# Token-outermost block transposes, a strided stationary operand, and one scattered row set per slot, in a two-layer gated cross-attention kernel

## The reference, cut to what matters

```python
# second attention: 16 heads of width 128, 8 key/value heads, softmax over 128 context tokens
scores = jnp.einsum('bhtd,bhsd->bhts', q, k) / scale
attn   = jax.nn.softmax(jnp.where(mask, scores, -jnp.inf), axis=-1)
out    = jnp.einsum('bhts,bhsd->bhtd', attn, v).transpose(0, 2, 1, 3).reshape(B, T_text, N_HEADS * HEAD_DIM) @ Wo
x = x + jnp.tanh(g_xattn[1]) * out
# second feed-forward: one shared expert, and 8 routed experts of which each token takes the best two
rw, sel = jax.lax.top_k(probs, 2)
x = x + jnp.tanh(g_ffn[1]) * (shared_out + sparse_out)
```

## Time and profile before

| | value |
|---|---|
| median of 3 runs | 1303.56 us (1302.22 to 1304.45) |
| the profiled execution: its own time | 1302.48 us |
| its span in the trace | 1300.7 us |
| PE busy | 1240.1 us, 95% |
| PE weight loads busy | 1098.9 us, 84% |
| DVE busy | 894.9 us, 69% |
| ACT busy | 738.5 us, 57% |
| POOL busy | 549.1 us, 42% |
| mean granted clock of PE | 0.989 |

### The profile page before, as it was taken

How to read it: one execution, slowest core, us unless ns; L and a number is a source line. 1 busy time by engine, 2 the same in 40 slices (tenths; PEclk the granted TensorE clock), 3 DMA queues, 4 the chain that set the end, 5 groups by cost and what they waited for, 6 DMA issues and landing times. The chain is left out here.

```text
span 1300.7 us, 23370 instructions
## 1 busy us (share of the span) xinstructions
PE 1240.1 (95%) x7907; PEld 1098.9 (84%) x7907; DVE 894.9 (69%) x2453; ACT 738.5 (57%) x2053; POOL 549.1 (42%) x542
## 2 busy tenths in 40 slices
PE   6899999999999989999999989999999988999998
PEld 4788888888888878888888888899988977888987
DVE  6678788887988776743433346657687776788857
ACT  4777787777877743322222247666565653546542
POOL 3564456644565533200000001866668675223430
PEclk9999999999999989999999999999999998999999
DMA  7000000000000310398100011434343355413434
GB/s 266 10 1 1 9 1 1 1 9 0 0 0 1 74 31 2 113 326 245 64 0 1 1 18 49 142 112 136 100 138 130 115 179 166 118 45 99 129 100 174
DMA packets 85672, 101.09 MB, mean 78 GB/s; under 512 B 16985, under 2 KB 72802, under 8 KB 85186
## 3 DMA queue, kind: packets, MB, share of 16 engines
q1 hardware_dynamic: 82162, 90.45, 23.1%
q0 software_dynamic: 3408, 9.34, 2.0%
HBM read 53.60 MB, written 46.18 MB: 77 GB/s over the span
## 5 line engine op out<-in xcount | busy, mean ns | idle before, releaser
L98 PE MATMUL bank<-wvo_hi,pc_hi_a 128*128 128x256 f32 x512 | 149.7, 292 | 6.5 <-DVE pc_lo_a L1337 5.7
L1748 ACT ACTIVATE act_g_f<-bank 128x512 f32<-128x512 f32 x64 | 38.2, 598 | 190.9 <-PE bank L100 190.9
L100 PE MATMUL bank<-wvo_hi,pc_lo_a 128*128 128x256 f32 x512 | 144.8, 283 | 0.0
L99 PE MATMUL bank<-wvo_lo,pc_hi_a 128*128 128x256 f32 x512 | 144.6, 283 | 0.0
L1807 DVE TENSOR_TENSOR hid_f<-act_g_f,bank 128x512 f32<-128x512 f32 x64 | 44.0, 688 | 142.3 <-ACT act_g_f L1748 142.3
L877 ACT ACTIVATE probs_a<-bank,nbias_a,q_r_a 128x128 f32<-128x128 f32 x256 | 114.4, 472 | 23.7 <-DVE nbias_a L995 23.4
L140 POOL TENSOR_TENSOR rstd<-mv,half 128x4 f32<-128x4 f32 x12 | 12.2, 1020 | 260.7 <-DVE mv L135 260.7
L1055 POOL TENSOR_TENSOR probs_a<-probs_a,rden_a 128x512 f32<-128x512 f32 x64 | 66.6, 1041 | 103.8 <-DVE rden_a L1001 103.8
L98 PEld LDWEIGHTS bank<-wvo_hi,pc_hi_a 128*128 128x128 f32 x512 | 98.2, 192 | 12.5 <-DVE pc_lo_a L1337 8.3
L1277 ACT ACTIVATE probs_a<-probs_a,nmin_a 128x128 f32<-128x128 f32 x256 | 99.5, 392 | 7.7 <-DVE nmin_a L1321 7.4
L99 PEld LDWEIGHTS bank<-wvo_lo,pc_hi_a 128*128 128x128 f32 x512 | 98.5, 192 | 3.2
(11 more groups left out here) (314 smaller groups left out, 4139.9 us busy)
## 6 DMA issues: line engine op xcount, KB each, us to landing
rows_in<-blank_f SPq DMA_DIRECT2D x8, 2193.0 KB, 21.1
staged<-blocks_a SPq DMA_DIRECT2D x32, 512.0 KB, 2.9
turned_a<-staged SPq DMA_DIRECT2D x128, 128.0 KB, 2.9
xs_raw_f<-rows_in SPq DMA_DIRECT2D x39, 129.0 KB
y_tok_f<-rows_out SPq DMA_DIRECT2D x4, 1024.0 KB, 8.9
we_raw<-in_L_ffn_We_gate_up SPq DMA_DIRECT2D x2, 1408.0 KB, 9.9
ctx_raw_a<-in_ctx SPq DMA_DIRECT2D x8, 256.0 KB, 3.0
x_sb<-in_x SPq DMA_DIRECT2D x4, 512.0 KB, 10.1
```

Source lines behind the costliest of these rows:

```text
L98: nc.tensor.matmul(out, w[0], x[0], start=start, stop=False)
L99: nc.tensor.matmul(out, w[0], x[1], start=False, stop=False)
L100: return nc.tensor.matmul(out, w[1], x[0], start=False, stop=stop)
```

## The change

Four things are changed, all in the second attention and the routing.

1. `blocks` and `turned` hold a block's 128 columns as (token, head), head innermost. TV therefore writes each element four words (16 bytes) behind the one before. Th and Tl become plain copies of 128 x 512 without rearrangement. The columns of `pt`, of C's result and of `pc` are now (token, head), and W's stationary operand for head h is every fourth element of `pc`.
2. SC is one indirect DMA for a word, not two. Groups 0 and 1 have their eight words in slots 35 to 42 and in slots 51, 52, 53 and 58 to 62; before they had them in pairs in slots 35 to 38 and 51 to 54. Group 2's eight words stay in slot 0 of the feed-forward stage and group 3's in slot 7.
3. Group 2's routing (`hurried`) stands earlier from NA on: RT, RL and RS by one slot, all other words by two (the last, PL, at 29 instead of 31).
4. The last unit's TV stands at the end of slot 57, before SH; before it stood in slot 58, behind SH.

The diff, cut to its core:

```diff
@@ second_order
     routing = {15: "E0", 17: "E1", 20: "NA0", ...
-               30: "RQ0", 32: "RQ1", 33: "RK0", 34: "PL0 PL1", 35: "SC0", 36: "SC1", 37: "SC2", 38: "SC3"}
-    hurried = {15: "E0", 17: "E1", 20: "NA0 NA1", 21: "NA2 NA3 NM0", 22: "NB0 NB1", 23: "NB2 NB3", 24: "NX0 NX1", 25: "RT0 RL0", 26: "RS0",
-               28: "RQ0", 29: "RQ1", 30: "RK0", 31: "PL0 PL1"}
+               30: "RQ0", 32: "RQ1", 33: "RK0", 34: "PL0 PL1"}
+    scatter = [{35 + n: f"SC{n}" for n in range(8)}, {51: "SC0", 52: "SC1", 53: "SC2", 58: "SC3", 59: "SC4", 60: "SC5", 61: "SC6", 62: "SC7"}]
+    hurried = {15: "E0", 17: "E1", 18: "NA0 NA1", 19: "NA2 NA3 NM0", 20: "NB0 NB1", 21: "NB2 NB3", 22: "NX0 NX1", 24: "RT0 RL0", 25: "RS0",
+               26: "RQ0", 27: "RQ1", 28: "RK0", 29: "PL0 PL1"}
...
-        unit(v - 1, "TV")
+        if v < U:
+            unit(v - 1, "TV")
...
+        for r in range(2):
+            words(scatter[r].get(s, ""), r)
         unit(s, "Ch", "Cl")
...
+        if v == U - 1:
+            unit(v, "TV")
         words(following.get(s, ""))
@@ second_attention
-        pc = pair("pc", [P, 2, QH, P])
+        pc = pair("pc", [P, 2, P, QH])
...
-                        last = three_pass(nc, out_of(b), [v[:, n % 2, h, :] for v in pc], [v[:, j * QH + h, :] for v in w["vo"]],
+                        last = three_pass(nc, out_of(b), [v[:, n % 2, :, h] for v in pc], [v[:, j * QH + h, :] for v in w["vo"]],
...
-                    nc.vector.transpose(blocks[:, p % 2, :, n % 2, :].rearrange("p j (h t) -> p h j t", h=QH),
+                    nc.vector.transpose(blocks[:, p % 2, :, n % 2, :].rearrange("p j (t h) -> p h j t", h=QH),
...
-                    nc.gpsimd.tensor_copy(pt[0][:, n % 2, :].rearrange("p (h i t) -> p i h t", h=QH, i=4),
-                                          turned[:, n // 2 % 2, :, n % 2, :].rearrange("p i (h t) -> p i h t", h=QH)).then_inc(sem("pt_hi_ready"), 1)
+                    nc.gpsimd.tensor_copy(pt[0][:, n % 2, :].rearrange("p (i x) -> p i x", i=4), turned[:, n // 2 % 2, :, n % 2, :]).then_inc(sem("pt_hi_ready"), 1)
@@ Router.gpsimd_step
-            b = m * GB + i
+            b, r = m * GB + i // 2, i % 2
             pool.wait_ge(self.places_ready, m + 1)
-            for r in range(2):
-                self.scatter(self.pay[:, b, :], self.row_of[:, r, b:b + 1], self.rows_in[:, :], self.rows_sent)
+            self.scatter(self.pay[:, b, :], self.row_of[:, r, b:b + 1], self.rows_in[:, :], self.rows_sent)
```

More of the change, by code:

```diff
@@ L1367, in _ @@
                         pool.wait_ge(sem("c_filled"), n - 1)
-                    nc.gpsimd.tensor_copy(pt[0][:, n % 2, :].rearrange("p (h i t) -> p i h t", h=QH, i=4),
-                                          turned[:, n // 2 % 2, :, n % 2, :].rearrange("p i (h t) -> p i h t", h=QH)).then_inc(sem("pt_hi_ready"), 1)
+                    nc.gpsimd.tensor_copy(pt[0][:, n % 2, :].rearrange("p (i x) -> p i x", i=4), turned[:, n // 2 % 2, :, n % 2, :]).then_inc(sem("pt_hi_ready"), 1)
                 elif name == "Tl":
                     pool.wait_ge(sem("pt_hi_ready"), n + 1)
-                    hi, lo = (v[:, n % 2, :].rearrange("p (h i t) -> p i h t", h=QH, i=4) for v in pt)
-                    nc.gpsimd.tensor_tensor(lo, turned[:, n // 2 % 2, :, n % 2, :].rearrange("p i (h t) -> p i h t", h=QH), f32(hi),
-                                            ALU.subtract).then_inc(sem("pt_ready"), 1)
+                    hi, lo = (v[:, n % 2, :].rearrange("p (i x) -> p i x", i=4) for v in pt)
+                    nc.gpsimd.tensor_tensor(lo, turned[:, n // 2 % 2, :, n % 2, :], f32(hi), ALU.subtract).then_inc(sem("pt_ready"), 1)
         return {"weights_used": (sem("w_done"), U), "scores_read": (sem("min_ready"), U), "probs_read": (sem("pt_ready"), U),
@@ L2136, in routed_feed_forward @@
     extras = {
[1 row of a table removed]
+        0: ["NB 3 0", "NB 3 1", "NB 3 2", "NB 3 3", *(f"SC 2 {n}" for n in range(8))],
         1: ["X 1 0", "X 1 1", "SD 0", "SD 1", "SD 2"],
@@ L2143, in routed_feed_forward @@
         6: ["RK 3", "SE 2", "SE 3"],
[1 row of a table removed]
+        7: ["PL 3 0", "PL 3 1", *(f"SC 3 {n}" for n in range(8)), "SE 4"],
         8: ["TB 0"],
```

## The result

| | before | after |
|---|---|---|
| median | 1303.56 us (1302.22 to 1304.87, 5 runs) | **1371.3 us** (1369.46 to 1373.46, 5 runs) |
| span of the profiled execution | 1300.7 us | 1371.7 us |
| mean granted clock | 0.989 | 0.989 |

The ratio is 1.0522, 95% interval 1.0508 to 1.0537: the change costs 68 us. I had forecast 1293, range 1286 to 1310. The second attention carries 70.0 of the 71.0 us between the two spans. Its first C starts at 815.94 us before and 816.94 after, and the next stage's first matmul, which ends it, at 1108.56 and at 1179.52: 292.6 and 362.6 us. The feed-forward stage behind it lasts 192.1 and 192.2 us.

What follows compares the result with a forecast made beforehand. PE, busy 95% of the span, was taken as the bound. From 1302.48 us, -1.8 (group 0's scatters), -10 (tail) and +1 (transpositions) gave 1291.7; with the median 1.1 us higher, 1293 us, range 1286 to 1310.

Steps and rivals of the forecast that it cites:

- W's stationary operand: W's loads at every fourth element, second attention: taken as 0, from no cost to twice the load, +67 us.
- 13% of cover: W's load of at most 0.100 us lies under 0.113 us of moving columns, hidden until 13% dearer.
- Rival A: Strided loads are dear and bound every W, with no cover: 1321 us at 1.5 times, 1360 at twice; chance 0.17.
- Group 0's scatters -1.8: Slots with Q: one scatter each fits PE's slot, so the 1.82 us wait for Tl goes; -1.8 us.
- the tail -10: 1051.5 to 1108.5 us: waits for Tl, low clock and late transposition avoidable; -10 us, best -14, worst -4.
- The routing words: Group 2's moved RT, RL, RS and others were said to hold the same work; no separate gain was booked.
- The chain behind unit 63's transposition: End of the second attention: the late transposition's 2.6 us counted as avoidable by moving it ahead of SH.
- What is late next: In the tail DVE was named next in line, 43 us if transpositions are dear, plus some 4 us closing chain.
- The 5 us of clock: Tail: PE's work at the low clock, 13.7 us at the low level, counted as 5 us of avoidable loss.
- Transpositions +1: DVE's writes 16 bytes apart take 0.685 to 1.22 us each, mostly hidden; +1 us, bounds 0 and 3.
- DVE's dense stretches: 950 to 970 and 1030 to 1050 us, where dearer transpositions would bring DVE to 20.6 and 19.8 us.
- Th and Tl as plain copies 0: POOL's copies without rearrangement save nothing: 0, with -0.2 us a slot as best case in POOL-bound slots.

Runs made afterwards that it cites:

- experiment 3: Kernel before with one edit: W reads its stationary operand at every fourth element (16 bytes apart), on wrong columns; 1373.1 us, ratio 1.0531.
- Experiment 8: Kernel before with transpositions writing 16 bytes apart, Th and Tl gathering every fourth element, W's loads contiguous; 1320.1 us, ratio 1.0129.
- step 2: Kernel before with W's stationary operand read at every second element (8 bytes apart), wrong columns; 1308.3 us, ratio 1.0028.
- experiment 1: Changed kernel with the four layout places as before, so only the new order remains; 1291.7 us, ratio 0.9908.
- experiment 4: Changed kernel with Ch and Cl putting the heads apart while copying, so W reads unbroken columns; 1295.9 us, ratio 0.9938.
- experiments 2 and 3: The first of the two: kernel before with the new layout in its four places, in the old order; 1375.1 us, ratio 1.0544.
- steps 3 and 8: Kernel before, W's stationary operand at every third element (1338.7 us), or every eighth, taken from the output weights (1379.8 us).

## Why the prediction was wrong, point by point

- **The step that failed is the term "W's stationary operand": I took 0, bounds 0 and +67.** It is +84.5 us gross and +70 us in the time of experiment 3, which has this load alone, both outside my upper bound. Two things were wrong in it. The upper bound took "twice the load", 0.200 us; the load is 0.235 us, 2.35 times the 0.100, which is itself only a bound on a contiguous load. And the value was chosen by L1839 as the nearest strided row, another engine's. I took from its 2.2 ns an element that a step costs nothing. It has 384 elements with a conversion in it, against one with 512 and none, and so it proved nothing about steps. Experiment 8 shows that on POOL itself a step of 16 bytes costs Th 0.50 us. PEld at 84% and 17.92 of 20 us stood in the rows I used. Load records overlap (193 ns each, 113 ns apart), so that share is no measure of the room, but with a full PE and 13% of cover an unmeasured cost may not be put at nothing.
- **Rival A had the mechanism right** ("every W is then bound by its load, with no cover, since PE is full"; from 0.113 us on), and 0.17 was too little for it. Its argument against, that a load asks half of what moving data gets, was about columns. What the five steps follow is the groups of 16 bytes touched. Its multiplier was a little high: 704 loads, not 768, since the first of each unit lies under C.
- The Trainium skill's page Advanced Engine Details and Errata, section SBUF Cachelines, had this rule: 16-byte lines, and two hits on a line needed to absorb the latency. The runs agree: two hits (step 2) leave 0.117 us, one (step 4) 0.235. I had set the rule aside because it names no price. A rule that speaks against a term with 13% of cover needs only the sign.
- **Group 0's scatters -1.8 and the tail -10: right as a sum** (11.8 against 11.4 measured in experiment 1), with the share off. The scatters carry 10.2. Group 0's part was 2.3 us (unit 40's C starts 181.4 instead of 183.7 us behind the first C). Of the rest the waits for Tl are the named part that went (9.0 to 2.4 us); how much the clock gave by itself no run shows. The routing words, which I had booked as the same work, bring 4.1 us alone. The chain behind unit 63's transposition, which I counted with 2.6 us among the avoidable, is worth nothing alone. So it is in part luck that the sum came out so well. What is late next was named rightly: DVE, with Cl.
- **In the changed kernel the order gives only 3.8 us** by the medians, because longer PE slots cover the same waits. I had not written that a dear load would also eat the gain: rival A's 1360 kept all of it. The account of the two profiled executions: the loads are 84.5 us by count, of which PE's busy time shows 82.4; less the 11.4 us of idle time that PE no longer has (mainly the 9.0 behind Tl and 3.1 of the 5.7 behind Cl) that makes the 71 us of the spans. The 5 us of clock that I counted did not come back on the whole: the mean is 0.989 in both. The last 59.5 us of the stage have 0.94, better than the 0.88 of before, but there are dips elsewhere (below).
- **Transpositions +1, bounds 0 and 3:** 1.085 us each lies inside the 0.685 to 1.22 that I gave, and the cost is 4.2 us with quick loads (the intervals of the two ratios allow some 1.5 to 6.5) and some 2 without, which is not clear of noise. The term was likely too small: DVE's dense stretches were counted, its place in the tail, where most of the 4 us arise (experiment 4), was not.
- **Th and Tl as plain copies 0:** right, 617 and 1290 ns against 621 and 1292.

## What to carry to other kernels

Look at the step of a stationary operand as at its size: in this kernel a load of 128 fp32 columns was all but free up to a step of two and took 1.83 ns for each 16 bytes touched above that, and it is hidden only under matmuls that are longer. If a layout must be interleaved, take it apart where the operand is copied out of PSUM: ACT's and DVE's strided reads there took the time of contiguous ones. And a gain from removed waits is not to be added to a term that lengthens the slots in which those waits stood.

## What the runs showed of the hardware that I had not expected

- A stationary load's cost by step: 0.117, 0.175, 0.235 and 0.242 us for steps 2, 3, 4 and 8, so it hardly grows beyond four elements (step 8 reads another tile).
- Reading PSUM at every fourth element costs neither ACT (584 ns) nor DVE (686 ns) anything. POOL's read of SBUF with the same step costs 0.50 us in Th's copy of 128 x 512 (1120 against 621 ns) and 0.28 us in Tl's subtraction, and DVE's transposition that writes SBUF with it 0.40 us.
- PE's clock falls in places where its records show no hole. Stretches of 4 us in after:

```profile
974.00:978.00 4.00, 4.00 (x26) 4.00 (x24) 0.90 (x7) 0.48 (x4) 1.89 (x2) 1.00 0.04 7
978.00:982.00 4.00, 4.00 (x18) 3.42 (x18) 2.41 (x7) 1.74 (x6) 0.93 (x1) 0.59 0.02 4
```

Ahead of it stood the W's of a unit, 0.235 us apart, and sixteen matmuls of nine columns. Then the 512-column matmuls of Q start 0.43 us apart instead of 0.23, at 1.2 GHz, until 982.4. A second dip, 1111.8 to 1115.4 us, stands behind such W's and eight matmuls of 8 to 32 columns. In before the same narrow matmuls stand behind W's 0.113 us apart (938.54 us), and no stretch of 4 us from 816 to 1048 us is below 1.00. In the body of the stage, dips under a full PE are in all five kernels with loads of 0.175 us or more (after, experiments 2 and 3, steps 3 and 8), and in none of before, experiments 1 and 4, step 2, the scatters or the routing alone. So a PE that is held by its loads is busy in the records and still can lose the clock. That is a link between traces; no run tested the cause by itself.
